# Batch 1's gated layer moved into the first projections' waits, packing put ahead of the later weight loads, and the last two periods written out in an order of their own

## The reference

```python
# layer 0, gated by the batch's domain
h = gelu(x @ down_W.T + down_b)
h = (h @ expert_W[dom].T + expert_b[dom]) + domain_emb[dom]
x = layernorm(h @ up_W.T + up_b + x) * ln_gamma + ln_beta
# layer 1, attention of 16 heads of 16 features, with a given 256x256 bias per head
x = layernorm(x) * (1 + scale[step]) + shift[step]
p = softmax(where(mask, -inf, q @ k.T / 4 + attention_bias))
x = x + (p @ v) @ Wo + bo
h = layernorm(x) * g2 + beta2
x = x + gelu2(h @ W1 + b1) @ W2 + b2
# layer 2, one of three networks by the batch's kind
y = x + (gelu(x @ w1 + b1) @ w2 + b2)     # kind 2 has one more product
x = layernorm(y) * gamma + beta
# layer 3, finite differences of x times fixed grids, in both directions
df = -(grad_rows(A0*x) + grad_cols(A1*x)) + 0.5*(grad2_rows(B0*x) + grad2_cols(B1*x) + 2*grad_rows(grad_cols(B2*x)))
out = maximum(x + df * dt, 0)
```

## Time and profile before

| what | value |
|---|---|
| median of 3 runs | 883.87 us (882.42 to 885.88) |
| the profiled execution | 884.87 us, its span 883.1 us |
| PE busy | 816.8 us, 92% |
| DVE busy | 737.9 us, 84% |
| ACT busy | 621.9 us, 70% |
| POOL busy | 163.7 us, 19% |
| the chain that ended last | PE 85%, DVE 9%, issue 2%, ACT 1%, DMA 1% |
| HBM read and written | 98.23 and 4.23 MB |

### The profile page before, as it was taken

One profiled execution on the slowest core, in us unless ns is written; L12 is line 12 of the kernel. 1 busy time (PEld: TensorE's weight loads), 2 busy tenths in 40 slices (PEclk: granted clock), 3 DMA queues, 4 the chain that ended last, 5 costly groups with the idle time before them and its releaser, 6 DMA issues.

```text
span 883.1 us, 18591 instructions
## 1 busy us (share of the span) xinstructions
PE 816.8 (92%) x5968; PEld 698.2 (79%) x5968; DVE 737.9 (84%) x2474; ACT 621.9 (70%) x1284; POOL 163.7 (19%) x160
## 2 busy tenths in 40 slices
PE   5568999999999999999999999999999999998791
PEld 2447678888888898888888888888888888787581
DVE  5664777898989899898989898998989898969555
ACT  2244767887878787878778787878787887777230
POOL 3010102222122203031211222030302112201200
PEclk9667999999999999999999999999999999999996
DMA  5942879576776756576766767595857576591110
GB/s 176 276 125 85 171 184 203 139 175 162 161 184 168 196 137 170 152 195 155 174 162 169 185 156 192 138 187 147 186 158 174 157 166 166 139 203 43 54 36 12
DMA packets 147593, 137.33 MB, mean 156 GB/s; under 512 B 19282, under 2 KB 144787, under 8 KB 147492
## 3 DMA queue, kind: packets, MB, share of 16 engines
q1 hardware_dynamic: 147172, 135.80, 61.9%
q10 hardware_dynamic: 320, 0.26, 0.1%
HBM read 98.23 MB, written 4.23 MB: 116 GB/s over the span
## 4 chain that ended last, share of the span: by engine, by line
PE 85%; DVE 9%; issue 2%; ACT 1%; DMA 1%; POOL 0%; SPq 0%; POOLq 0%; DVEq 0%
PE back_bank L1115 13%; PE turn_bank L1071 12%; PE context_bank L1125 7%; PE score_bank L1192 7%; PE score_bank L1193 6%; PE front_bank L1109 5%; PE back_bank L1109 5%; PE attend_bank L1109 5%; PE front_bank L1142 4%; PE back_bank L1095 3%; PE front_bank L1298 3%; PE back_bank L1086 3%; PE attend_bank L1095 3%; PE attend_bank L1056 2%; PE front_bank L1346 2%
## 5 line engine op out<-in xcount | busy, mean ns | idle before, releaser
L549 ACT ACTIVATE sc<-sc,negmax 128x256 f32<-128x256 f32 x512 | 231.2, 504 | 21.9 <-DVE negmax L911 21.4
L911 DVE CUSTOM_DVE_ANT_0 sc<-score_bank,side 128x256 f32<-128x256 f32 x512 | 195.5, 420 | 37.0 <-PE score_bank L1193 33.0
L526 ACT ACTIVATE pt<-turn_bank 128x512 f32<-128x512 f32 x176 | 105.9, 602 | 133.9 <-PE turn_bank L1071 112.8
L1071 PE MATMUL turn_bank<-ident,sc 128*128 128x128 f32 x1024 | 157.9, 277 | 1.1 <-ACT sc L549 1.0
L1071 PEld LDWEIGHTS turn_bank<-ident,sc 128*128 128x128 f32 x1024 | 123.8, 142 | 31.9 <-issue 13.7
L1192 PE MATMUL score_bank<-ks,qs 128*128 128x256 f32 x512 | 124.1, 324 | 7.2 <-DVE negmax L911 6.7
L1115 PE MATMUL back_bank<-w,ffT 128*128 128x256 f32 x512 | 118.0, 379 | 0.0
L1115 PEld LDWEIGHTS back_bank<-w,ffT 128*128 128x128 f32 x512 | 97.0, 190 | 12.7
L1193 PE MATMUL score_bank<-mask_neg,ident_r 128*128 128x512 f32 x256 | 103.1, 403 | 0.0
L466 POOL TENSOR_TENSOR rstd<-var,half_neg 128x2 f32<-128x2 f32 x64 | 49.9, 780 | 272.6 <-DVE var L836 271.0
L1192 PEld LDWEIGHTS score_bank<-ks,qs 128*128 128x128 f32 x512 | 79.4, 195 | 16.1 <-DVE negmax L911 9.1
(11 more groups left out here) (217 smaller groups left out, 1975.4 us busy)
## 6 DMA issues: line engine op xcount, KB each, us to landing
side<-in_side SPq DMA_DIRECT2D x128, 512.0 KB, 5.4
qs<-qh SPq DMA_DIRECT2D x128, 64.0 KB, 4.3
qs<-ql SPq DMA_DIRECT2D x128, 64.0 KB, 4.1
ks<-kl SPq DMA_DIRECT2D x128, 64.0 KB, 4.3
wb<-in_wb SPq DMA_DIRECT2D x16, 512.0 KB, 7.1
ks<-kh SPq DMA_DIRECT2D x124, 64.0 KB, 3.8
xN<-in_x SPq DMA_DIRECT2D x16, 256.0 KB, 5.0
wc<-in_wc SPq DMA_DIRECT2D x16, 256.0 KB, 3.0
```

Of the source, the lines that this page charges most:

```text
L526: e.activation(pt[:, h % NP2, :, :], two(tbank[h % 2]), ACT.Copy).then_inc(copied[h % 4], 1)
L549: i = e.activation(sc[:, h % NS, q, :], sc[:, h % NS, q, :], ACT.Exp, bias=negmax[:, q, h:h + 1], scale=-1.0)
L911: i = e.tensor_tensor_reduce(sc[:, s % NS, q, :], two(sbank[s % 2])[:, q, :], side[:, (H * X.i + s) % NSIDE, q, :], -1.0, 3.4e38, ALU.add, ...
L1071: i = e.transpose(tbank[h % 2][:, k * S + q * P:k * S + q * P + P], sc[:, h % NS, q, k * P:k * P + P], ident[:, :])
```

## The change

**Gated layer of batch 1.** In period -1 its steps move: turn of `xN` to slot 3, `down` to slot 5, `expert` to slot 6 behind the Q product, `up` to slot 7 behind the K product, all into `back_bank`; DVE's sum and statistics to slot 8, POOL's power to slot 9. Other periods keep theirs. The first ada product gets a semaphore of its own, ahead of the rows' product.

**Packing and loads.** `load_rest` moves from period -1, slot 1, to period 0, slot 1, behind all packing of batch 0 and behind the next x, expert and mask loads. SP no longer waits for the `ada_rows` store in slot 4, but ahead of half 1's packing in slot 9, where it also loads `ada` for batch 1. In period 0 the eight K packings of batch 1's half 0 move from SP (slots 9 to 12) to ACT (slot 8). What uses the loads moves too: ACT's scaling of `w2` to period 0, slot 8, and DVE's preparations from slots 11 and 12 of period -1 and slots 1 to 7 of period 0 to slots 7 to 14 of period 0. The first bias's 16 small products on PE (with `w1_raw`, rows L1176 before) move from slot 9 to slot 3 of period 0, DVE's use of them from slot 11 to slot 5.

**The last two periods.** From period 16 on, PE, ACT and DVE leave the slots and run `last_turns`, with the same work in another order; period 18's work becomes the end of it. Batch 15's `wb` goes to a place in `sc` (`wb_last`), free by then, and is loaded in slot 2 of period 16.

```diff
@@ SP @@
-                    if is_step(t, s, -1, 1):
+                    if is_step(t, s, 0, 1):
                         load_rest()
                     if is_step(t, s, -1, 4):
                         e.wait_ge(dve_set, ADA_SET)
                         e.dma_start(d["ada_rows"], x3T[0:NB, :, :]).then_inc(st_ada, 16)
-                        e.wait_ge(st_ada, 16)
...
                         for m, blocks_ in ((0, range(NBLK)),) if s == 8 else ((0, (1, 3)), (1, range(NBLK))):
+                            if m == 1:
+                                e.wait_ge(st_ada, 16)
+                                load_ada(G)
...
                         pack_q(e, m, b, u)
-                        pack_k(e, m, b, u)
+                        if (x.i, m) != (1, 0):
+                            pack_k(e, m, b, u)
@@ ACT, slot 8 @@
+                        if t == 0:
+                            e.wait_ge(ev["kl_ready"], F.n)
+                            e.wait_ge(ev["kh_ready"], F.n)
+                            head(e, scored, X, HM - 1)
+                            for b in range(NBLK):
+                                for u in range(2):
+                                    pack_k(e, 0, b, u)
...
-                    if is_step(t, s, -1, 11):
-                        e.wait_ge(ld_bo, 3 * 16)
+                    if is_step(t, s, 0, 8):
+                        e.wait_ge(ld_late, 7 * 16)
                         e.activation(w2[:, :, :], w2[:, :, :], ACT.Copy, scale=0.5).then_inc(act_set, 1)
@@ PE, last_turns, period 16 @@
+                second_ff(T, ((1, 0), (1, 1), (1, 2), (1, 3), (0, 4), (0, 5)), no_more)
+                four(flips(B, H - 2))
+                four(flips(B, H - 1))
+                second_ff(T, ((0, 6), (0, 7), (1, 4)), no_more)
+                mix(B, 3)
+                gather(B, 0, ev["c1_lo"])
+                second_ff(T, ((1, 5), (1, 6), (1, 7)), no_more).then_inc(ev["w2_done"], 1)
+                gather(B, 1, ev["c1_hi"])
+                differ(U, 0)
+                turn(abank, ctxN, ev["c2_turned"])
+                differ(U, 1)
+                project(abank, ctxT, wo, ev["wo_done"], no_more)
+                turn(bbank, x3, ev["x3_turned"])
+                condition(T, kind, wb)
+                turn(abank, n3, ev["n3_turned"])
+                project(bbank, gbT, wc, ev["c_done"], no_more)
+                for j, bank in enumerate(LAST_BANKS):
+                    project_T_parts(bank, w1, w1l, 2 * P * j, n3h, n3l, 2, ev["w1_done"])
+                second_ff(B, ((0, 0), (0, 1), (0, 2), (0, 3)), no_more)
@@ DVE, last_turns, the end of period 17, for x in (U, T) @@
+                        product_r2(T)
+                        inner_u(T)
+                        product_r1(T)
+                        sum_u(T)
+                        low_r2(T)
+                        low_u(T)
+                    grid_product(x, t_a, grid_a, "ga_ready")
+                    grid_product(x, t_b, grid_b, "gb2_ready")
+                    grid_product(x, t_c, grid_c, "gc_ready")
+                    inner_e(x)
+                    sum_e(x)
+                    sum_w(x)
+                    step_w(x)
```

More of the change, by code:

```diff
@@ L364, in load_side, with load_ada @@
                             ).then_inc(ld_side[c], 16)
+            def load_ada(x):
+                wait(e, ev["x1_ready"], x.p)
+                e.dma_start(ada[:, :, :].rearrange("p a n -> p (a n)"), d["ada_rows"][bass.ds(x.i, 1)].rearrange("b n -> (b n)").partition_broadcast(P)).then_inc(ld_ada, 16)
             def stack(x, prev, m, blocks):
@@ L526, in copy_turned, with exponentials, copy_context_hi @@
                 e.activation(pt[:, h % NP2, :, :], two(tbank[h % 2]), ACT.Copy).then_inc(copied[h % 4], 1)
+            def exponentials(x, h):
+                head(e, biased, x, h)
+                for q in range(TT):
+                    i = e.activation(sc[:, h % NS, q, :], sc[:, h % NS, q, :], ACT.Exp,
+                                     bias=negmax[:, q, h:h + 1], scale=-1.0)
+                i.then_inc(expd[h % 4], 1)
+            def copy_context_hi(x):
+                mixes(e, x, 3)
+                e.activation(cts[:, 2:4, :], two(cbank), ACT.Copy).then_inc(ev["ct_hi"], 1)
@@ new lines, in copy_context, with high_n3, first_ff @@
+            def copy_context(x):
+                e.wait_ge(ev["c2_turned"], x.n)
+                e.activation(ctxT[:, :, :], two(abank), ACT.Copy).then_inc(ev["ctxT_ready"], 1)
+            def high_n3(x):
+                e.wait_ge(ev["n3_turned"], x.n)
+                e.activation(n3h[:, :, :], two(abank), ACT.Copy).then_inc(ev["n3T_ready"], 1)
+            def first_ff(x, j, bank):
+                quarter(e, "w1_done", x, j)
+                for m in range(2 * j, 2 * j + 2):
+                    i = e.activation(ffT[:, m, :], two(bank)[:, m % 2, :], ACT.Identity, bias=b1c[:, m:m + 1])
+                i.then_inc(ev["u1_ready"], 1)
@@ new lines, in sum_x3, with step_w @@
+            def sum_x3(x):
+                e.wait_ge(ev["w2_done"], x.n)
+                e.wait_ge(ev["x2b_ready"], x.n)
+                wait(e, ev["x4_ready"], x.p)
+                e.tensor_tensor(x3[:, :, :], two(bbank), x2b[:, :, :], ALU.add).then_inc(ev["x3_ready"], 1)
+            def step_w(x):
+                e.wait_ge(ev["w_ready"], x.n)
+                e.scalar_tensor_tensor(out=t_e[:, :, :], in0=t_e[:, :, :], scalar=dt[:, bass.ds(x.i, 1)], in1=fN[:, :, :],
+                                       op0=ALU.mult, op1=ALU.add).then_inc(ev["w2s_ready"], 1)
@@ new lines, in differ_when_ready @@
+            def differ_when_ready(x):
+                for m, parts, ready in ((d2T, (r2_h, r2_l), "r2l_ready"), (d1T, (u_h, u_l), "ul_ready")):
+                    e.wait_ge(ev[ready], x.n)
+                    for q in range(TT):
+                        for k in range(KT):
+                            for n, part in enumerate(parts):
+                                i = e.matmul(two(fbank)[:, q, :], m[:, k, q * P:q * P + P], part[:, k, :], start=(m is d2T and q == 0 and k == 0 and n == 0),
+                                             stop=(m is d1T and q == TT - 1 and k == KT - 1 and n == 1))
+                i.then_inc(ev["d_done"], 1)
@@ L1342, in body @@
                             project_T_parts(bbank, w1, w1l, 4 * P, n3h, n3l, 2, ev["w1_done"])
-                        if G:
-                            e.wait_ge(ev["g1_ready"], G.n)
-                            for q in range(TT):
-                                i = e.matmul(two(fbank)[:, q, :], g1[:, q * P:q * P + P], upT[:, :], start=True, stop=True)
-                            i.then_inc(ev["up_done"], 1)
+                        if G and t != -1:
+                            up(G, fbank)
                         for n in range(4):
```

488 lines of the change are left out of this document (335 added, 153 removed).

## The result

The changed kernel takes **876.1 us** (median of 4 runs, 875.6 to 876.48) where the kernel before, run beside it, takes 884.27 (882.42 to 885.88). The ratio is 0.9908, with a 95% interval of 0.9887 to 0.9928. The forecast was 871, the range 863 to 878. The profiled execution took 875.6 us with a span of 873.7; its busy times are those of before within 1 us but for TensorE (810.6 us in place of 816.8), and its granted clock over the whole span is 0.972 in place of 0.96.

What follows compares the result with a forecast made beforehand. TensorE was taken to run without a gap in the middle, leaving waits in the opening and closing. 884.87 less 3.5 (opening) and 9.3 (closing) gave 872.1; the profiled execution stood 1.0 above the median, so 871 us, range 863 to 878.

Steps and rivals of the forecast that it cites:

- the rival that gave 875: Opening gives nothing: side load lands at 72 or later, or ScalarE's 7.1 us count in full; chance 0.16.
- Packing first: Opening: SP packs without waiting for the `ada_rows` store; first score at 43.6 against 51.01, 7.4 us gained.
- The loads and the side load: Opening: twelve loads start at 54.6, head 6 starts at 68.8; of the 7.4 us, 1.3 are left.
- ScalarE's slot 8: Batch 0: `w2` scaling 1.90 us, eight packings 5.2; head 10's score at 84.5 against 89.62, 5.1 gained.
- The grid work: Opening, slots 9 to 14: about 7 us of DVE cost an estimated 2 us beyond idle time filled.
- Opening 3.5: Whole opening: 3.5 us gained, between 0 (stall eats all) and 8.5 (side load in time).
- Period 16: Closing: `wo` ahead of conditional layer and `wc`; batch 15's second products end at 847.9 against 853.86, 6.0 us gained.
- The meeting with GpSimd, 1.0: Closing, about 838: GpSimd's `b2r` addition meets VectorE's scale of `x4`, with gates behind it; 1.0 us taken off.
- The last chain, 3.3: After `x4`: low halves made first, so 3.5 us of DVE run beside TensorE's products; saves 3.3 us.
- What would show it: Signs: first score near 43.6, loads 54 to 63, DVE idle about 7 us, last score to end 62 us.
- The rival that was to make the kernel slower: Head 6's side load late: 888 us and more, all 12.8 us gone at a landing about 81.6; chance 0.05.
- the first four cases: Forecast 0.48, opening gives nothing 0.16, opening keeps its lead 0.16, closing's waits move 0.12; sum given as 0.91.

Runs made afterwards that it cites:

- Removing VectorE's wait alone: Changed kernel with SP's later weight loads behind the side loads of heads 6 to 9 (slot 5 of batch 0, not slot 1): 876.91 us, ratio 0.9924.
- the opening alone: Changed kernel with its closing undone, batch 16's two last periods in the common slots again: 886.6 us, ratio 1.0031.
- three moves around `wo`: Changed kernel with the contexts' second turn and `wo` behind the conditional layer again, `wc` ahead of `wo` and `n3`'s turn: 883.34 us, ratio 0.9999.
- its own run: Changed kernel with batch 16's low halves of r2 and u made last, TensorE's derivatives chunk by chunk: 880.38 us.
- the setups behind the contexts: Kernel with loads in batch 1's period and bias product spread; loads now behind batch 1's side loads, setups in its slots 9 to 15: 867.26 us.
- K on SP: Changed kernel with the eight K packings of batch 1 back from ScalarE to SP: 869.66 us, ratio 0.9843.

## Why the prediction was right, and where not

The time lies in the range, but 5.1 us above the forecast. The closing came as it was worked out. The opening went by the rival that gave 875 and had a chance of 0.16: head 6's side load landed later than 72 us, and all of the lead was gone.

- **Packing first:** right. 44.11 against 43.6 forecast.
- **The loads and the side load:** this is the term that was mis-sized. The wait was foreseen, its size not. VectorE asked at 61.3 (61 forecast). SP took 7.6 us for the twelve loads (7.5 forecast), but began them at 56.18, not 54.6, so the side load was issued at 63.85, not 62.3. It took 9.2 us to landing, not 6.5, and head 6 began at 73.15 and not 68.8, 4.35 us late and 3.05 later than in the old kernel. I had priced the landing by the 6.8 us of the earlier trace rows. No packing was on its way beside it (the last was issued at 52.48). The rate dipped to 145 and 164 GB/s between 68 and 70 us; why, no run shows.
- **ScalarE's slot 8:** sized right, but late by what head 6 was late. The sum had eight packings of 5.2 us end at 80.2; they took 5.1 and ended at 85.12. It gave 5.1 us at head 10's score; that came at 87.99, 1.6 earlier than before. What the prediction did not ask is whether this term had to be paid at all: with K's packings on SP, 6.4 us come back. Removing VectorE's wait alone gave nothing, as the same loads then held ScalarE.
- **The grid work:** 2 us forecast; the 1.6 us left at head 10 were gone at batch 1's first scores. How much of it the setups took was not tested.
- **Opening 3.5:** measured 0 by the traces, −2.5 by the medians of the opening alone.
- **Period 16:** right in each mark. `wo` 825.62 (825.65), `n3` 831.15 (831.8), second products 839.74 (839.9). The second products end at 847.53, 6.3 us before those of the earlier trace rows, where 6.0 were given. The faster pace of the first feed-forward products, 1.4 in the sum, is there too: 24 of them took 3.03 us, and 4.4 in the earlier trace rows. Undoing the three moves around `wo` cost 7.2, more than the 6.3: the new order of the rest is worse than the old without them.
- **The meeting with GpSimd, 1.0:** right for VectorE (1.89 against 0.88), somewhat high for the chain. TensorE's second products took 0.7 us longer in its presence, with waits for two of VectorE's gates; the last six waited for gate 3, as the sum had it, until 844.67.
- **The last chain, 3.3:** `x4` at 855.42 (855.5), the order 3.3 by its own run.
- **The sum:** 884.87 less 9.5 for the closing is 875.4; the profiled execution took 875.6.
- **What would show it:** the loads between 56 and 64 and not 54 and 63, VectorE idle 11.8 us and not 7, packings near 80 and not 76, head 0 of batch 1 at 103 and not 99; 61.3 us from the last score to the end (61 to 62 forecast), TensorE's last gap 9.08.

The rival that was to make the kernel slower, with all gains gone at a landing at 81.6, came a third of the way: head 6 began 4.35 us late of the 12.8. By my own count that should have left the opening at about −1; it left 0. In the chances, the first four cases add up to 0.92, not 0.91.

## What to carry to other kernels

When a lead is won ahead of a burst of loads, ask what the burst meets next, and go on asking. Here some engine waited 5 to 12 us for it wherever it stood, and moving that one wait alone gave nothing. A DMA issue that is put on a busy engine costs what is queued behind it (eight issues of 0.64 us on ScalarE: 6.4 us), however idle that engine is on average. At the end of a kernel, where one chain is left, order alone paid: the chain's own product, with its turn, ahead of a conditional layer was worth 7.2 us, about 2 of them by the clock behind the idle time that it took away, and low halves ahead of independent products 3.3.

## What the runs showed of the hardware

**DMA rate.** With packings and loads together the DMA engines were busy 1.11 of the time (queues' packet time over the span) at 241 and 262 GB/s, in the two rows of the kernel with the setups behind the contexts. With loads alone they reached 362 at 1.10, from 62 to 64 us in the changed kernel:

```profile
62.00:64.00 2.00, 2.00 (x26) 1.25 (x26) 0.00 (x0) 0.84 (x2) 0.00 (x0) 1.00 1.10 362
```

**Time to landing.** The `w2` load took 6.3 us in the changed kernel, where the DMA engines were busy only 0.39 of the time as it was issued, and 10.2 us in the kernel with the setups behind the contexts, where packings stood beside it (a line of each one's DMA view; KB, then the median to landing):

```profile
w<-in_w SPq DMA_DIRECT2D x1, 1024.0 KB, 6.3
```

```profile
w<-in_w SPq DMA_DIRECT2D x1, 1024.0 KB, 10.2
```

It took the same 10.2 us in the kernel before, behind other loads and with no packing near. So a full queue alone is enough, and the runs don't show what the packings added.

**Small matmuls and the clock.** The 32 one-column matmuls took 6.83 us in the changed kernel, where the stretch from 44 to 54 us shows the granted clock at 0.50, its lower level of 1.2 GHz. In the kernel with K on SP the same ones took 3.77 us, at a granted clock of 0.99 (changed kernel, then K on SP):

```profile
44.00:54.00 10.00, 9.88 (x42) 9.08 (x42) 6.70 (x25) 3.20 (x7) 0.70 (x1) 0.50 0.35 104
```

```profile
48.00:51.50 3.50, 3.50 (x32) 3.50 (x33) 3.21 (x14) 2.29 (x5) 0.70 (x1) 0.99 0.31 108
```

TensorE had waited 3.54 us before its first score in the one and 3.93 in the other, so the wait just before doesn't tell the two apart.
